# Two-slot periods for TensorE in the attention part, rotations one slot later, query sums on VectorE

## The reference, cut to what matters

```python
xn = layernorm(x)                                  # x: 8 sequences of 256 tokens, 128 features
q = rope(xn @ wq.T)                                # 16 heads of 64
kv = xn @ w_kv_down.T                              # 64 latent features
k, v = rope(kv @ w_k_up.T), kv @ w_v_up.T
probs = softmax(causal(q @ k.T / sqrt(64)))        # for each head
s = concat_heads(probs @ v) @ wo.T
e = max(top2(xn @ gate_w + gate_b))                # one expert of 8 for each token
g = silu(2 * (gelu(xn @ w1[e] + b1[e]) @ w2[e] + b2[e]))
out = x + s * g
```

## Time and profile before

| | |
|---|---|
| median of 3 runs | 305.51 us (305.35 to 305.71) |
| the profiled execution | 305.23 us, span 303.5 us |
| PE busy | 290.1 us (96% of the span) |
| PEld busy | 234.8 us (77%) |
| DVE busy | 227.1 us (75%) |
| ACT busy | 243.2 us (80%) |
| POOL busy | 217.2 us (72%) |
| PE in the chain that ended last | 66%; POOL 12%, issue 8%, DVE 6% |
| granted TensorE clock | 9 tenths or more in all 40 slices |

### The profile page before, as it was taken

How to read it: one execution, slowest core, us unless ns; L and a number is a source line. 1 busy time by engine, 2 the same in 40 slices (tenths; PEclk the granted TensorE clock), 3 DMA queues, 4 the chain that set the end, 5 groups by cost and what they waited for, 6 DMA issues and landing times.

```text
span 303.5 us, 8596 instructions
## 1 busy us (share of the span) xinstructions
PE 290.1 (96%) x2362; PEld 234.8 (77%) x2362; DVE 227.1 (75%) x905; ACT 243.2 (80%) x871; POOL 217.2 (72%) x321
## 2 busy tenths in 40 slices
PE   8897999999999999999999999999999999899994
PEld 3665888888888888777777789999877777676763
DVE  4889998987786998988888524444398899897651
ACT  4387889898977789989898677777779989799982
POOL 3468878687777779999999963333158999899730
PEclk9999999999999999999999999999999999999999
DMA  6854594979433333333334490000513344344200
GB/s 203 251 132 116 104 297 116 236 172 303 101 68 65 67 77 83 101 88 98 89 88 109 96 288 6 2 2 0 154 38 83 100 120 117 93 115 123 61 19 17
DMA packets 39596, 33.35 MB, mean 110 GB/s; under 512 B 4801, under 2 KB 36674, under 8 KB 39554
## 3 DMA queue, kind: packets, MB, share of 16 engines
q1 hardware_dynamic: 38098, 30.51, 39.1%
q0 software_dynamic: 1024, 2.10, 2.5%
q10 hardware_dynamic: 432, 0.23, 0.3%
HBM read 11.07 MB, written 4.98 MB: 53 GB/s over the span
## 4 chain that ended last, share of the span: by engine, by line
PE 66%; POOL 12%; issue 8%; DVE 6%; DMA 3%; ACT 2%; SPq 2%; POOLq 1%; DVEq 0%; ACTq 0%
PE bank L1128 9%; PE bank L1116 9%; PE bank L1142 8%; PE bank L1339 7%; PE bank L1156 6%; PE bank L1327 6%; POOL probs L477 4%; POOL staged L466 4%; PE bank L1090 4%; PE bank L1144 3%; PE bank L1118 3%; DVE masked L602 2%; PE bank L1106 2%; POOL xn L493 2%; DMA z<-in_woT 2%
## 5 line engine op out<-in xcount | busy, mean ns | idle before, releaser
L906 ACT ACTIVATE pexp<-masked,negmax 128x128 f32<-128x128 f32 (+1 forms) x256 | 114.1, 453 | 2.2 <-DVE negmax L602 2.2
L477 POOL TENSOR_SCALAR probs<-pexp,rden 128x256 f32<-128x256 f32 (+1 forms) x184 | 80.3, 451 | 24.3 <-DVE rden L609 21.7
L602 DVE CUSTOM_DVE_ANT_0 masked<-bank,mask 128x128 f32<-128x128 f32 (+1 forms) x256 | 75.9, 352 | 25.2 <-PE bank L1118 25.0
L466 POOL TENSOR_TENSOR staged<-rot_out 128x512 f32<-128x512 f32 x63 | 80.1, 1273 | 17.5 <-DVE rot_out L593 16.9
L593 DVE TENSOR_TENSOR rot_out<-bank,rot 128x1024 f32<-128x1024 f32 x64 | 77.6, 1214 | 3.9 <-PE bank L1092 2.7
L928 ACT COPY probsT<-bank 128x384 f32<-128x384 f32 x128 | 55.0, 481 | 23.8 <-PE bank L1128 22.8
L1128 PE MATMUL bank<-ident,probs 128*128 128x128 f32 x384 | 54.1, 275 | 1.3 <-POOL probs L477 0.6
L906 ACT ACTIVATION_READ_ACCUMULATOR pexp<-masked,negmax 128x1 f32 x256 | 50.0, 195 | 0.0
L1116 PE MATMUL bank<-qk_sb 64*128 64x256 f32 x256 | 45.0, 427 | 3.2 <-DVE negmax L602 2.5
L1128 PEld LDWEIGHTS bank<-ident,probs 128*128 128x128 f32 x384 | 43.1, 140 | 4.1 <-issue 1.5
L1156 PE MATMUL bank<-vo_sb,ctxT 128*128 128x128 f32 x256 | 39.5, 279 | 0.7 <-ACT ctxT L935 0.7
(11 more groups left out here) (114 smaller groups left out, 485.6 us busy)
## 6 DMA issues: line engine op xcount, KB each, us to landing
qk_sb<-staged SPq DMA_DIRECT2D x128, 128.0 KB, 2.7
w_sb<-in_w SPq DMA_DIRECT2D x2, 1024.0 KB, 6.1
w_sb<-in_w SPq DMA_DIRECT2D x4, 512.0 KB, 4.8
sorted_x<-z SPq DMA_DIRECT2D x1, 1408.0 KB, 8.0
sorted_g<-z SPq DMA_DIRECT2D x1, 1152.0 KB, 5.9
out<-res SPq DMA_DIRECT2D x8, 128.0 KB, 1.9
x_sb<-in_x SPq DMA_DIRECT2D x3, 256.0 KB, 3.3
rot<-in_c_rot SPq DMA_DIRECT2D x1, 512.0 KB, 5.8
```

The costliest lines, as they stand in the source:

```text
L466: pool.tensor_tensor(staged[:, n % 2, :, m % 2, :], rot_out[:, m % 2, :, 0:S], rot_out[:, m % 2, :, S:2 * S], op=ALU.add).then_inc(staged_ ...
L477: pool.tensor_scalar(probs[:, g % 2, i, c], pexp[:, g % 2, i, c], rden[:, g % 2, i, k:k + 1], 1.0, ALU.mult, ALU.mult).then_inc(probs_read ...
L602: t = dve.tensor_tensor_reduce(masked[:, g % 2, i, c], s_bank[i][:, c], mask[:, c], -1.0, -NEG * 1e8, ALU.add, ALU.min, negmax[:, g % 2, i ...
L906: e = act.activation(pexp[:, g % 2, i, c], masked[:, g % 2, i, c], ACT.Exp, bias=negmax[:, g % 2, i, k:k + 1], scale=-1.0, accum_out=rowsu ...
```

## The change

- **TensorE's order.** In slots 26 to 37 and 42 to 57 TensorE goes by periods of two slots s, s + 1 (`PERIODS`, `period`): scores of s + 2, values of s - 2 and s - 1 (none in period 42), scores of s + 3, transposes of s, a query projection, the outputs of s - 2 and s - 1, transposes of s + 1, a key projection. Between the two scores there was a projection, transposes, an output and in even slots the values; now there are the values alone.
- **The wait of scores.** `scores(g)` waits for each of its two banks by itself, where it waited for both ahead of the first.
- **Rotations.** In these slots VectorE rotates the projections of the slot before, right behind the row maximum, where it rotated those of the same slot at the slot's end. For queries it then adds the halves itself (a tensor_tensor with both inputs in SBUF, 128x512); for keys GpSimd goes on doing it. `staged_ready` becomes two semaphores.
- **Scaling.** In these slots VectorE's piece goes to GpSimd, which has three of the four, two of them 128x256.
- **Tables.** The slots with two projections are 22 and 24, not 36 and 38, so that projections are 8 slots ahead from slot 25 on. Scatters stand in 22, 24, 26 to 37, with two in 29 and 33 and none in 23 and 25. `finalise(5)` stands in slot 50, not 51, and every finalise waits for the one before.
- **Contexts.** ScalarE copies the contexts of a period behind both exponentials of its even slot.

```diff
-TWICE = (36, 38)
+TWICE = (22, 24)
-FINALS = {48: 0, 51: 5, 53: 1, 54: 2, 56: 3, 59: 6, 61: 4}
+FINALS = {48: 0, 50: 5, 53: 1, 54: 2, 56: 3, 59: 6, 61: 4}
+PERIODS = (*range(26, G_LEAD - 2, 2), *range(G_LEAD + 2, B * NP - 6, 2))
+def rotations(g):
+    behind = items(g - 1) if in_period(g - 1) else []
+    return [*behind] if in_period(g) else [*behind, *items(g)]
+VECTOR_SUMS = tuple(m for g in range(B * NP) if in_period(g) for m in items(g) if m % 2 == 0)
...
-            return "pool" if k or not busy else ("vector", "scalar")[i]
+            return "pool" if k or not busy else ("pool" if in_period(g - 1) else "vector", "scalar")[i]
...
             def rotate(m):
...
+                if m == 1 or m in VECTOR_SUMS:
+                    n = m // 2
+                    dve.wait_ge(rope_done, m + 1)
...
+                    dve.tensor_tensor(staged[:, n % 2, :, m % 2, :], rot_out[:, m % 2, :, 0:S], rot_out[:, m % 2, :, S:2 * S],
+                                      op=ALU.add).then_inc(staged_ready[m % 2], 1)
...
             def finalise(b):
                 k = FINAL_ORDER.index(b)
+                wait(dve, res_ready, k)
...
-                wait(pe, masked_ready, 2 * g)
                 for i, r in enumerate(half_rows):
+                    wait(pe, masked_ready, 2 * g - 1 + i if g else 0)
                     pe.matmul(s_bank[i][:, P:SW], qk_sb[r, 0, p, P:S], qk_sb[r, 1, p, :], start=True, stop=True)
...
+            def period(s):
+                scores(s + 2)
+                if s != G_LEAD + 2:
+                    values(s - 2)
+                scores(s + 3)
+                turn(s)
+                for m in items(s)[:1]:
+                    project(m)
+                if s - 2 not in PERIODS and s - 3 not in ALONE:
+                    output(s - 3)
+                output(s - 2)
+                output(s - 1)
+                turn(s + 1)
+                for m in items(s + 1):
+                    project(m)
+                for m in items(s)[1:]:
+                    project(m)
```

More of the change, by code:

```diff
@@ L67, in items, with in_period @@
     return range(g + ahead[0], min(g + 1 + ahead[1], B * NP))
+def in_period(g):
+    return g - g % 2 in PERIODS
+def rotations(g):
+    behind = items(g - 1) if in_period(g - 1) else []
+    return [*behind] if in_period(g) else [*behind, *items(g)]
+VECTOR_SUMS = tuple(m for g in range(B * NP) if in_period(g) for m in items(g) if m % 2 == 0)
 def host_constants():
@@ L256, in build @@
         rope_done = sem("rope_done")
-        staged_ready = sem("staged_ready")
+        staged_ready = [sem(f"staged_ready{i}") for i in range(2)]
         qk_in = [sem(f"qk_in{p}") for p in range(NP)]
@@ L298, in scaler @@
         def scaler(g, i, k):
-            busy = SCATTER_SLOT <= g - 1 < SCATTER_SLOT + NT or GATHER_SLOT <= g - 1 < GATHER_SLOT + NT
+            busy = g - 1 in SCATTERS or GATHER_SLOT <= g - 1 < GATHER_SLOT + NT
             if g == 0 or g >= B * NP - 3:
                 return ("vector", "pool")[i]
-            return "pool" if k or not busy else ("vector", "scalar")[i]
+            return "pool" if k or not busy else ("pool" if in_period(g - 1) else "vector", "scalar")[i]
         def take_turns(eng, g, i, k):
@@ L359, in place @@
             def place(n):
-                sp.wait_ge(staged_ready, 2 * n + 2)
+                for i in range(2):
+                    sp.wait_ge(staged_ready[i], n + 1)
                 wait(sp, scores_done, 2 * n + 2 - NP)
@@ L466, in rotated @@
                 pool.tensor_tensor(staged[:, n % 2, :, m % 2, :], rot_out[:, m % 2, :, 0:S], rot_out[:, m % 2, :, S:2 * S],
-                                   op=ALU.add).then_inc(staged_ready, 1)
+                                   op=ALU.add).then_inc(staged_ready[m % 2], 1)
             def scale(g):
@@ L539, in slot @@
                     first_weights()
-                for m in items(g):
-                    rotated(m)
-                if SCATTER_SLOT <= g < SCATTER_SLOT + NT:
-                    scatter(g - SCATTER_SLOT)
+                for m in rotations(g):
+                    if m not in VECTOR_SUMS:
+                        rotated(m)
+                for n in range(NT):
+                    if SCATTERS[n] == g:
+                        scatter(n)
                 if GATHER_SLOT <= g < GATHER_SLOT + NT:
@@ L591, in rotate @@
                 dve.wait_ge(proj_done, m + 1)
-                wait(dve, staged_ready, max(m - 1, 2) if m > 1 else 0)
+                wait(dve, staged_ready[m % 2], m // 2)
                 dve.tensor_tensor(rot_out[:, m % 2], bank_of(m)[:].unsqueeze(1).broadcast_to([P, 2, 2 * S]), rot[:],
                                   op=ALU.mult).then_inc(rope_done, 1)
+                if m == 1 or m in VECTOR_SUMS:
+                    n = m // 2
+                    dve.wait_ge(rope_done, m + 1)
+                    for q in (2 * n - 4, 2 * n - 3) if n > 1 else ():
+                        dve.wait_ge(qk_in[q % NP], 32 * (q // NP) + 32)
+                    dve.tensor_tensor(staged[:, n % 2, :, m % 2, :], rot_out[:, m % 2, :, 0:S], rot_out[:, m % 2, :, S:2 * S],
+                                      op=ALU.add).then_inc(staged_ready[m % 2], 1)
             def row_max(g):
@@ L746, in start @@
                 rotate(1)
-                dve.wait_ge(rope_done, 2)
-                dve.tensor_tensor(staged[:, 0, :, 1, :], rot_out[:, 1, :, 0:S], rot_out[:, 1, :, S:2 * S],
-                                  op=ALU.add).then_inc(staged_ready, 1)
                 normalise(1)
@@ L793, in slot @@
             def slot(g):
-                if 0 < g // NP < LEAD and g % NP == (2 if NP * (g // NP) <= FIRST_DOUBLE else 3):
+                if 0 < g // NP < LEAD and g % NP == (2 if NP * (g // NP) <= FIRST_DOUBLE or in_period(g) else 3):
                     take_y(g // NP - 1)
@@ L807, in slot @@
                     gate_rows(NR - 1, 1)
+                if in_period(g):
+                    for m in rotations(g):
+                        rotate(m)
                 if g + 1 < B * NP and g != G_LEAD:
@@ L856, in slot @@
                     finalise(FINALS[g])
-                for m in items(g):
-                    rotate(m)
+                if not in_period(g):
+                    for m in rotations(g):
+                        rotate(m)
             def finish(b):
@@ L1038, in slot @@
                     ctx_out(g - 2)
-                if g % 2 and g > 2 and g - 3 not in ALONE and g not in (G_LEAD + 1, B * NP - 1):
+                if g % 2 and g > 2 and g - 3 not in ALONE and g not in (G_LEAD + 1, B * NP - 1) and not in_period(g):
                     ctx_out(g - 3)
@@ L1042, in slot @@
                     exponentials(g + 1, 1)
+                if g in PERIODS:
+                    ctx_out(g - 2)
                 if g == B * NP - 2:
@@ L1256, in start @@
                 pe.wait_ge(lat_copied, 1)
+            def period(s):
[15 more added lines that the diff above has]
+                    project(m)
             def slot(g):
+                if in_period(g):
+                    if g in PERIODS:
+                        period(g)
+                    return
                 if g + 2 < B * NP:
@@ L1278, in slot @@
                     count_tokens()
-                if g > 2 and g - 3 not in ALONE and g not in (G_LEAD, G_LEAD + 1, G_LEAD + 2):
+                if g > 2 and g - 3 not in ALONE and g not in (G_LEAD, G_LEAD + 1, G_LEAD + 2) and g - 2 not in PERIODS:
                     output(g - 3)
```

2 lines of the change are left out of this document (1 added, 1 removed).

## The result

The changed kernel takes **312.15 us** (median of 4 runs, 311.34 to 312.88), the kernel before in the same comparison 305.61 (305.35 to 306.38): ratio 1.0209, 95% interval 1.0177 to 1.0241. It is 2.1% slower where 0.5% faster was forecast, and above the range. The profiled execution took 311.34 with a span of 309.6, so the two spans (303.5 before) differ by 6.1 us, and the rest of this text divides these 6.1.

A forecast was written before the change was run, and what follows sets the result against it. TensorE was taken as the bound, GpSimd nearly as full. Changeovers -3.15, period 42 +0.65, old stalls -2.75 and new stalls +3.9 make -1.35 us, from 305.51 to 304.1 us; range 301.6 to 308.8.

The forecast's parts named there:

- Changeovers: TensorE's switches between tile shapes: the new order saves 0.25 us a period, -3.15 us in all.
- values behind scores: TensorE's changeover from scores to values, in no row: bounded by 0 and 0.20 us more than behind an output, taken as 0.
- The rival of 306.7: Values behind scores pay both changeovers, so TensorE's work does not shorten: +2.6 us, 306.7; chance 0.08.
- Period 42: No values between its two scores, so the second waits 1.1 us for the row maximum, less 0.45 for changeovers: +0.65.
- The stalls of before: TensorE's waits at a late transfer and in slots 38, 52 and 56 end: 0.25 + 0.4 + 1.2 + 0.9, -2.75 us.
- A GpSimd that is no longer full: GpSimd with room to spare ends TensorE's stalls in slots 38 and 56, 0.4 and 0.9 us.
- New stalls: VectorE late from double scatters 0.7, slots 22 and 24 0.3, finalises 2.4, ScalarE without projections 0.5: +3.9 us.
- paid as before: Moved double projections cost in slots 22 and 24 what they cost in 36 and 38, 0.7 and 0.9 us.
- VectorE is locked out for GpSimd's whole run: Finalises beside GpSimd wait for its whole run of scalings and sum: +3.6 us, 309; chance 0.22.
- The finalises hide: VectorE catches up while TensorE waits, 0.8 for 2.4, and double scatters cost nothing: -3.6 us, 301.9; chance 0.16.
- VectorE the bound in every period: VectorE 0.25 us late at each second scores: +1.65 us, 307, or half of it, 305.6; chance 0.18.

The follow-up runs named there:

- e1: Changed kernel with SyncE's load of sorted_x put ahead of slot 37's placing of its query and key pair; 307.80 us.
- e3: Changed kernel with periods from slot 42 on only; scatters and double projections of slots 22 to 41 as in the kernel before; 305.80 us.
- e9: e3 with five filler products of ones on TensorE in slot 58; 305.61 us.
- e2: e1 with scatters in 22, 23 and one in each of 25 to 38, none in 24 and none double; 312.54 us.
- e8: Changed kernel with ten filler products of ones on TensorE ahead of the wait for the load, which stays late; 310.91 us.
- e4: e1 with slots 42 and 43 as an ordinary pair, the second stretch of periods starting at 44; 310.78 us.
- e5: e3 without period 56; 306.87 us.
- e7: e1 with VectorE's scaling in slots 22 and 24 on GpSimd, double scatters in 27 and 31, no period 56, slot 50's finalise behind the row maximum; 308.48 us.
- e6: e5 with the finalise of slot 50 behind that slot's row maximum; 306.86 us.
- e12: Kernel before, without periods, with slot 51's finalise moved behind its row maximum; 305.25 us, ratio 0.9981.

## Why the prediction was wrong

**The step that failed: the queues that a moved step is moved past.** The sum had terms for TensorE, VectorE, GpSimd and ScalarE, and none for SyncE; the expert part stood in it at zero. It followed the later rotations on VectorE, to GpSimd and to the transposes, and stopped there; who waits for their sums on SyncE it did not ask. The same edit, with the double projections moved, put a late key in front of SyncE's load. Slot 39 to 40, with the expert part, took 4.24 us longer, of the 6.1 in the traces. e1, which changes nothing but this order, gives 3.77 of them back, and its median is 4.35 us lower. Without it the changed kernel is 307.8: inside the range of 301.6 to 308.8, still on the wrong side of the forecast.

**Changeovers: right in mechanism, a fifth too large.** Predicted 0.25 a period, measured 0.20 (6.93 to 6.73) or a little more, in eight of the fourteen periods. The cost that no row showed, values behind scores, can now be read. The chain of e3 in period 46, scores, values, scores, transposes:

```profile
245.11 0.63 PE bank L1145 x4
245.74 0.22 PE bank L1147 x4
245.96 1.04 PE bank L1171 x4
247.00 0.43 PE bank L1173 x4
247.44 0.63 PE bank L1145 x4
248.07 0.22 PE bank L1147 x4
248.29 0.82 PE bank L1157 x6
```

Values behind scores take 1.04, where they took 1.01 behind an output: not both changeovers. The rival of 306.7 is out. By the eight the term was too large by 12 x 0.05 = 0.6 us; what the other periods lost is counted under the new stalls.

**Period 42: +0.65 predicted, +1.38 measured.** The second scores waited 0.84 for the first bank and again for the second, which a separate wait now makes possible:

```profile
232.67 0.95 PE L1145 MATMUL bank<-qk_sb 64*128 64x256 f32 x3 [0.84 <-DVE negmax L627]
...
233.46 0.38 PE L1145 MATMUL bank<-qk_sb 64*128 64x256 f32 x1
```

From the first of these products to the next group it is 1.31 us, where scores without a wait between their halves take 0.85, so the whole wait is 0.84 + 0.46, near the 1.1 that I took. What I left out is an output: the period has two of them, the pair had one, 0.45 us.

**The stalls of before, -2.75 predicted.** The late transfer (0.25) and the row maximum in slot 52 (1.2) went. The two that were laid to GpSimd did not: slot 38 still has a transposes group of 1.26 behind a wait of 0.50, and slot 58 has 1.27 in place of 0.62 in slot 56. "A GpSimd that is no longer full" was true of a period, and false of the slots around them, and slots 56 to 60 take the same in either order of TensorE where the clock stays up (12.68 before, 12.81 now, 12.83 in e9). ScalarE is busy for 10.63 of the 11 us from 282 on; that it and GpSimd set the pace there is argued, not shown.

**New stalls, +3.9 predicted.** The finalises were priced too high: 0.7 for slots 48 and 50 instead of 1.4, nothing for 53 and 54. None was held, 0.42 to 0.80 each (rows 9 had 2.12):

```profile
L813 DVE TENSOR_TENSOR res<-gated,x_sb x8: 424/489/798, 255.1 to 306.6; 128x256 f32<-128x256 f32 x8
```

The longest is in slot 58, beside two of GpSimd's scalings. The double scatters were priced too low, 0.7 for both: the one of slot 29 cost 0.26, the one of slot 33 1.07. And slots 22 and 24, which I let be "paid as before", lost 0.7 us more than their projections (2.30 against 1.6), and from slot 60 to the end, where the sum had nothing, 0.6 was lost. Slot 24 on TensorE, VectorE and GpSimd:

```profile
117.78 1.53 PE L1157 MATMUL bank<-ident,probs 128*128 128x128 f32 x6
...
118.70 1.45 DVE L645 TENSOR_SCALAR probs<-pexp,rden 128x128 f32<-128x128 f32 x1
118.79 1.27 POOL L482 TENSOR_TENSOR staged<-rot_out 128x512 f32<-128x512 f32 x1
```

**The rivals.** "VectorE is locked out for GpSimd's whole run" had the right mechanism at the wrong instructions. Not the finalises, but the scaling of slot 24 (1.45 for 0.29) and the query sum itself, which the change adds, were held:

```profile
L618 DVE TENSOR_TENSOR staged<-rot_out x14: 691/692/2578, 11.9 to 278.3; 128x512 f32<-128x512 f32 x14
```

The longest is in period 34, behind the double scatter: GpSimd runs three scalings and a sum one behind the other, and VectorE's sum, which starts in the second scaling, ends 0.56 us behind them all. In periods 30, 32 and 36 it took 1.82, 1.48 and 1.47; in 42 to 56 never more than 0.69.

```profile
155.92 0.96 POOL L501 DMA_INDIRECT sorted_x<-xn,pos  x1 [0.30 <-issue]
156.92 1.28 POOL L493 TENSOR_SCALAR probs<-pexp,rden 128x128 f32<-128x128 f32 x3
...
157.42 2.58 DVE L618 TENSOR_TENSOR staged<-rot_out 128x512 f32<-128x512 f32 x1
157.44 1.25 PE L1157 MATMUL bank<-ident,probs 128*128 128x128 f32 x6 [0.43 <-POOL probs L493]
158.17 1.27 POOL L482 TENSOR_TENSOR staged<-rot_out 128x512 f32<-128x512 f32 x1
```

The Trainium skill, page "SBUF — State Buffer", section "Who interferes with whom", which the prediction weighed, lets such an instruction wait for one of GpSimd's. These rows show it waiting for two scalings and a sum in a row. "The finalises hide" was right on the finalises: it had 0.8 for them in place of 2.4, and they cost 0.7. It was wrong on the double scatters, which it let cost nothing (1.33). "VectorE the bound in every period" named nothing that happened: it would have had TensorE wait at each second scores, and it did so in periods 42 and 50 alone.

**What the forecast named as its own test.** It was to fail as a whole if slots 26 to 37 were not shorter than 42.5 us. They took 41.75 and passed it by luck: 0.91 of the 42.5 was the second projection of slot 36, which the change moved out of the stretch. The test was also too narrow: it looked where the change was made, and the loss lies in the slots beside it (22 to 26, and 38 to 40).

## What to carry to other kernels

Where a change makes a result later, write down every queue in which something stands behind its use, SyncE's first, and ask of each what is next in it; one line of order there (3.77 us) cost more than fourteen periods gained (1.24 in both stretches, 0.91 of it a projection moved away). A regular stretch that gets shorter pays only if what enters and leaves it keeps pace: here most of what was saved came back as a wait for a gather, a scatter or a scaling in the next slots. And an order that leaves an engine no slack makes each neighbour's irregularity visible, so look for the single held instruction first, as in the kernel that won by moving one finalise.

## What the runs showed of the hardware

**A TensorE wait can cost twice, or once, and its length alone does not tell which.** Behind waits of 2.54 (changed), 3.10 and 1.75 (e2) and 1.65 us (e1, slot 58) the granted clock went to 0.50 for some three microseconds; behind 1.65 in the same slot of e8 and 1.19 (before) it stayed at 1.00. Behind 1.26 or 1.27 in slot 58 it fell in e3 and e4 and stayed up in the changed kernel and e2; behind two waits of 0.7 to 0.8 it fell in e5 and e7 and stayed up in e6. 0.50 is TensorE's lower level, 1.2 GHz of 2.4. In e1 that is seen from outside: of its eight executions, the four with a mean clock of 0.994 or less took 308.7 to 309.6, the four with 0.996 or more 306.5 to 306.9. Behind the wait for the load the same fall cost nothing in the traces, because the next thing needed was a DMA that took its 7 us at either clock (changed and e8).

**A VectorE instruction held beside GpSimd can wait for several of its instructions.** The sum of period 34 took 2.58 us for 0.69, the finalise of slot 51 before the change 2.12 for 0.42, and a scaling in e2 1.97 for 0.29, each until GpSimd's run of work was over.

**Still open.** The changed kernel and all eleven built on it need 0.5 to 0.6 us more from slot 60 to the end (18.14 to 18.25 against 17.65 and 17.64 in the kernel before and e12). About half lies in slot 60 (4.29 against 4.03), where the scores are split by the new wait, the other half behind the start of the last finalise instruction (3.0 against 2.7 to the end); no run took these apart.
